# Summing over partitions on GpSimd instead of TensorE in the second stage of a gated feed-forward kernel

## The chip, the cores and the metric

The kernel runs on one core of one Trainium2 chip. Its time is the device time of one execution in microseconds (us); the profile shows one such execution, engine by engine: PE is TensorE, DVE is VectorE, ACT is ScalarE, POOL is GpSimd, SP is SyncE, which here only issues transfers.

## The reference

```
xr = x.reshape(B, T, 8, 128)                       # B, T = 4, 1024
h = gelu(einsum('btel,elf->btef', xr, W1) + b1)    # 8 groups, 128 -> 512
y = (einsum('btef,efl->btel', h, W2) + b2).reshape(B, T, 1024)
scale, shift = split(silu(emb) @ emb_W + emb_b, 2)
mu  = mean(y, axis=-1)
var = mean(square(y - mu), axis=-1)
hn  = ((y - mu) * rsqrt(var + 1e-5) * ln_g + ln_b) * (1 + scale) + shift
out = x + silu(hn) @ out_W + out_b
```

All is float32. A float32 product is done as three products of rounded halves (high x high, high x low, low x high), so that operands are split into a high and a low part first.

## The kernel before, in words

Stage one (to about 367 us) works on 32 items of 1024 tokens of one group: the two small products, Gelu between them, and a store of y to memory, transposed so that the 1024 features of a token lie over 128 partitions times 8 groups.

Stage two works on 16 blocks p of 256 tokens. A block is a tile `yb` of 128 partitions x 8 groups x 256 tokens; there are three such tiles, used in turn. The mean and the variance of a token are sums over 8 groups and 128 partitions. The sum over groups is a tree of three additions on DVE into a tile `total` of 128 x 256 (`mean_sum_first`, `mean_sum_rest`, L540 to L550; for the squares `var_sum_first`, `var_sum_rest`, L567 to L573). The sum over partitions is a product on PE with a 128 x 128 tile `ones_r` that holds 1/1024, so that every partition gets the mean (L780, L781, `row_sum`). Since the product takes rounded operands, DVE first splits `total` into `sum_hi` and `sum_lo` (`mean_split_up` L554 and L556, `var_split_up` L577 and L579).

The loop over i runs on each engine in an order written out by hand, with semaphores between engines. In step i:

- PE does projections q = 2i and 2i + 1 (128 tokens each, 48 products of 512 columns, L847) on block i. Behind the last group of the first it puts the mean product of block i + 2, behind the second the variance product of block i + 2. A projection waits for `finish(q - 2)`, since it writes the PSUM pair that this frees, and for `s_lo` of its block.
- DVE, in this order: `finish(2i - 1)` (L694: projection + residual), the reciprocal of the standard deviation of block i + 1 (L588), its two halves of `norm` (L593), the tree of the mean of block i + 2 and its split, `rest_s` (L611: the low part of the activations, first half), `finish(2i)`, `centre` of block i + 2 (L562, subtracts the mean, two halves), `rest_s` second half, the tree of the variance of block i + 2 and its split.
- ACT: Silu of block i + 1 (L456), its rounding (L387), the squares of block i + 2 (L382), the table of the square root (L390), the square root (L396), the table of Silu (L464).
- GpSimd adds the output bias to a residual tile, q = 2i and 2i + 1 (L343). Add q waits for projection q - 1 to be done and for the load of the residual; `finish(q)` waits for it.

Blocks 0 and 1 take their sums in stage one, and the change leaves them as they are; blocks 2 to 15, 14 of them, take theirs in steps 0 to 13.

Of the kernel before, what the change touches and what calls it, by code (L numbers as in the profile page):

```python
# [5 lines left out]
P = 128  # L6
F32 = mybir.dt.float32
F32R = mybir.dt.float32r
ALU = mybir.AluOpType
ACT = mybir.ActivationFunctionType  # L10
# [5 lines left out]
def cond_ffn_program(nc, x, xT, vectors, W1, W2, emb_W, out_W, out_b, out):  # L16
    B, T, D = x.shape
# [6 lines left out]
    TP = 2 * P  # L24
    NP = B * T // TP
    PT = TA // TP
    QN = 2 * NP
    HG = G // 2
# [6 lines left out]
    N = len(ORDER)  # L35
# [18 lines left out]

    MEAN_ITEM = {23: 0, 25: 1}
    VAR_ITEM = {26: 0, 28: 1}
    MEAN_OF = {(p - 2, 0, 7): p for p in range(2, NP)}
    VAR_OF = {(p - 2, 1, 7): p for p in range(2, NP)}

    def act_rounds(m):  # L60
        return m % C in (3, 0)
# [14 lines left out]
    with ExitStack() as ctx:  # L76
# [3 lines left out]
        def at(name, shape, offset, dt=F32):  # L80
            return nc.alloc_sbuf_tensor_at(name, shape, dt, offset=BASE + offset)
# [4 lines left out]
        psum = ctx.enter_context(nc.psum_tensor("psum", [P, 8, BANK], F32))  # L86
# [4 lines left out]
        S0 = 64 * KB  # L91
# [11 lines left out]
        eps = at("eps", [P, 1], S0 + 5312)  # L103
        sum_hi = at("sum_hi", [P, TP], S0 + 5632, F32R)
        sum_lo = at("sum_lo", [P, TP], S0 + 6656, F32R)
        std = at("std", [P, TP], S0 + 7680)
        total = at("total", [P, TP], S0 + 8704)
        total1 = at("total1", [P, TP], S0 + 9728)
        rstd0 = at("rstd0", [P, TP], S0 + 1536)
        R0 = S0 + 10752  # L110

# [19 lines left out]
        sq = at("sq", [P, G, TP], R0 + 112 * KB)  # L132
# [85 lines left out]
        def proj(q):  # L218
            return pair(2 * (q % 2))

        mean_ps = psum[:, 4, 0:TP]
        rstd_ps = psum[:, 5, 0:TP]
        var_ps = psum[:, 7, 0:TP]

        def half_of(h):
            return slice(h * HG, (h + 1) * HG)
# [100 lines left out]
        @block.gpsimd  # L327
        def _(pool):
            nc.gpsimd.memset(ident[:], 0.0).then_inc(ident_zeroed, 1)
            pool.wait_ge(ident_zeroed, 1)  # L330
            nc.gpsimd.affine_select(out=ident[:], in_=ident[:], compare_op=ALU.not_equal, fill=1.0,
                                    base=0, pattern=[[-1, P]], channel_multiplier=1).then_inc(ident_ready, 1)

            pool.wait_ge(out_b_landed, 16)
            for q in range(QN):
                if q == 0:
                    pool.wait_ge(rstd_done, 2)
                else:  # L340
                    pool.wait_ge(proj_done, q)
                pool.wait_ge(res_landed[q % 4], 16 * (q // 4 + 1))
                nc.gpsimd.tensor_tensor(res[:, q % 4], res[:, q % 4], out_b_all[:], ALU.add).then_inc(res_biased, 1)  # L343

        @block.scalar
        def _(act):
# [39 lines left out]
                    act.wait_ge(proj_done, 2 * p - 2)  # L386
                nc.scalar.copy(s_hi[p % 2][:, half_of(h)], yb[p % 3][:, half_of(h)]).then_inc(shi_done, 1)  # L387

            def root(p, var):
                nc.scalar.preload_act_table(ACT.Sqrt)  # L390
                if p < 2:
                    act.wait_ge(var_copied, p + 1)
                act.wait_ge(var_done, p + 1)
                if p >= 1:
                    act.wait_ge(rstd_done, p)
                nc.scalar.activation(std[:], var, ACT.Sqrt, bias=eps[:]).then_inc(std_done, 1)  # L396

            def tanh_y0(h):
                act.wait_ge(y0_halved, (h + 1) * HG)
# [50 lines left out]
            for i in range(NP - 1):  # L450
                p = i + 1
                for h in range(2):
                    act.wait_ge(normed, 2 * p + h + 1)
                    for g in range(h * HG, (h + 1) * HG):
                        b = p // PT
                        nc.scalar.activation(yb[p % 3][:, g], yb[p % 3][:, g], ACT.Silu, scale=mod_a[:, b, g:g + 1],  # L456
                                             bias=mod_c[:, b, g:g + 1]).then_inc(silu_done, 1)
                    act.wait_ge(silu_done, G * i + (h + 1) * HG)
                    round_s(p, h)
                if p + 1 < NP:  # L460
                    square(p + 1, 0)
                    square(p + 1, 1)
                    root(p + 1, var_ps)
                    nc.scalar.preload_act_table(ACT.Silu)  # L464

        @block.vector
        def _(dve):
# [75 lines left out]
            def total_of(p):  # L543
                return (total1 if p == 1 else total)[:]

            def mean_sum_rest(p):
                dve.wait_ge(mean_tree, 3 * p + 1)
                nc.vector.tensor_tensor(sq[:, 0:2], sq[:, 0:2], sq[:, 2:4], ALU.add).then_inc(mean_tree, 1)
                dve.wait_ge(mean_tree, 3 * p + 2)
                nc.vector.tensor_tensor(total_of(p), sq[:, 0], sq[:, 1], ALU.add).then_inc(mean_tree, 1)  # L550

            def mean_split_up(p):
                dve.wait_ge(mean_tree, 3 * p + 3)
                nc.vector.tensor_copy(sum_hi[:], total_of(p)).then_inc(mean_split, 1)  # L554
                dve.wait_ge(mean_split, 2 * p + 1)
                nc.vector.tensor_tensor(sum_lo[:], total_of(p), sum_hi[:].bitcast(F32), ALU.subtract  # L556
                                        ).then_inc(mean_split, 1)

            def centre(p, h, mean):
                dve.wait_ge(mean_done, p + 1)  # L560
                part = yb[p % 3][:, half_of(h)]
                nc.vector.tensor_tensor(part, part, mean.unsqueeze(1).to_broadcast([P, HG, TP]), ALU.subtract  # L562
                                        ).then_inc(centred, 1)
# [5 lines left out]
            def var_sum_rest(p):  # L569
                dve.wait_ge(var_tree, 3 * p + 1)  # L570
                nc.vector.tensor_tensor(sq[:, 0:2], sq[:, 0:2], sq[:, 2:4], ALU.add).then_inc(var_tree, 1)
                dve.wait_ge(var_tree, 3 * p + 2)
                nc.vector.tensor_tensor(total_of(p), sq[:, 0], sq[:, 1], ALU.add).then_inc(var_tree, 1)  # L573

            def var_split_up(p):
                dve.wait_ge(var_tree, 3 * p + 3)
                nc.vector.tensor_copy(sum_hi[:], total_of(p)).then_inc(var_split, 1)  # L577
                dve.wait_ge(var_split, 2 * p + 1)
                nc.vector.tensor_tensor(sum_lo[:], total_of(p), sum_hi[:].bitcast(F32), ALU.subtract  # L579
                                        ).then_inc(var_split, 1)  # L580

            def copy_var(p, var):
# [113 lines left out]
            for i in range(NP):  # L696
                p, ahead = i + 1, i + 2
                if i > 0:
                    finish(2 * i - 1)
                if p < NP:  # L700
                    invert(p, rstd_ps)
                    norm(p, 0, rstd_ps)
                    norm(p, 1, rstd_ps)
                if ahead < NP:
                    mean_sum_first(ahead)
                    mean_sum_rest(ahead)
                    mean_split_up(ahead)
                if p < NP:
                    rest_s(p, 0)
                finish(2 * i)  # L710
                if ahead < NP:
                    centre(ahead, 0, mean_ps)
                    centre(ahead, 1, mean_ps)
                if p < NP:
                    rest_s(p, 1)
                if ahead < NP:
                    var_sum_first(ahead)
                    var_sum_rest(ahead)
                    var_split_up(ahead)
            dve.wait_ge(res_biased, QN)  # L720
            for h in range(2):
                half = slice(h * BANK, (h + 1) * BANK)
# [5 lines left out]
        def _(pe):  # L728
# [54 lines left out]
            def mean_of(p, ps):  # L783
                pe.wait_ge(mean_split, 2 * p + 2)
                row_sum(ps).then_inc(mean_done, 1)

            def var_of(p, ps):
                pe.wait_ge(var_split, 2 * p + 2)
                row_sum(ps).then_inc(var_done, 1)
# [73 lines left out]
            for i in range(NP):  # L863
                for t in range(2):
                    q = 2 * i + t
                    if q >= 2:
                        pe.wait_ge(out_ready, q - 1)
                    else:
                        pe.wait_ge(gelu_done, M - 1 + q)
                    if q == QN - 1:  # L870
                        project_halves(q)
                        continue
                    for g in range(G):
                        if t == 0 and g % HG == 0:
                            pe.wait_ge(slo_done, 2 * i + g // HG + 1)
                        project(q, g)
                        if (i, t, g) in MEAN_OF:
                            if i == 0:
                                pe.wait_ge(y_staged, N)
                            mean_of(MEAN_OF[i, t, g], mean_ps)  # L880
                        if (i, t, g) in VAR_OF:
                            var_of(VAR_OF[i, t, g], var_ps)

# [30 lines left out]
```

## Time and profile before

| | |
|---|---|
| median of 3 runs | 727.7 us (727.65 to 727.92) |
| profiled execution, its own time | 727.84 us |
| its span | 726.0 us |
| PE busy | 720.6 us (99%) |
| DVE busy | 552.2 us (76%) |
| ACT busy | 453.1 us (62%) |
| GpSimd busy | 77.9 us (11%) |

The span is what the profile shows between the first and the last instruction; the execution's own time is 1.84 us longer. Busy shares are means over both stages.

### The profile page before, as it was taken

The page shows a single profiled execution, that of the slowest core. Times are in us where ns is not written, and L with a number is a line of the kernel's source. Part 1 is how long each engine was busy: PE and PEld are TensorE (multiplying, and loading weights), DVE is VectorE, ACT ScalarE, POOL GpSimd, SP SyncE. Part 2 cuts the span into 40 slices and gives each one's busy share as a digit, 9 for nine tenths or more (in the row PEclk, how much of TensorE's full clock was granted, in tenths as well). Part 3 has the DMA queues.
Part 4 walks back from the last instruction along what each step waited for, and adds up shares of the span by engine and source line. Part 5 has one row for each costly group of instructions (what it writes and reads, how often), then busy time and mean ns, then how long its engine had stood idle before and what let it go on. Part 6 is the DMA issues. An engine that isn't in the chain of part 4 may idle for free.

```text
span 726.0 us, 8305 instructions
## 1 busy us (share of the span) xinstructions
PE 720.6 (99%) x3208; PEld 585.6 (81%) x3208; DVE 552.2 (76%) x627; ACT 453.1 (62%) x494; POOL 77.9 (11%) x38
## 2 busy tenths in 40 slices
PE   8999999999999999999999999999999999999998
PEld 5887778777787888888878888888888888888886
DVE  6887888788776788889887778778778777787521
ACT  7786777767777788897865455554456453555500
POOL 0000000000000000000021221212212212122121
PEclk9999999999999999999999999999999999999999
DMA  6335366554542713323173433334332344332221
GB/s 234 110 124 187 115 219 196 181 155 164 203 152 81 261 62 113 102 72 117 59 272 133 172 117 146 116 144 175 142 148 95 137 174 170 120 117 87 87 88 58
DMA packets 42471, 101.78 MB, mean 140 GB/s; under 512 B 3136, under 2 KB 23616, under 8 KB 39360
## 3 DMA queue, kind: packets, MB, share of 16 engines
q1 hardware_dynamic: 41760, 100.73, 39.3%
q10 hardware_dynamic: 672, 0.52, 0.2%
q8 instruction: 25, 0.41, 0.2%
q14 instruction: 14, 0.11, 0.0%
HBM read 67.69 MB, written 33.55 MB: 139 GB/s over the span
## 4 chain that ended last, share of the span: by engine, by line
PE 98%; DMA 1%; DVE 0%; ACT 0%; issue 0%; ACTq 0%
PE psum L847 47%; PE psum L740 24%; PE psum L756 24%; PE psum L859 2%; PE psum L766 1%; DMA wraw<-in_W 1%; PE psum L781 1%; PE psum L780 1%; PE psum L803 0%; DVE g_lo L515 0%; ACT g_hi L368 0%; DVE W L491 0%; DVE res L724 0%; DVE W L489 0%; PE psum L776 0%
## 5 line engine op out<-in xcount | busy, mean ns | idle before, releaser
L515 DVE TENSOR_TENSOR g_lo<-g_raw,g_hi 128x1024 fp32r<-128x1024 f32 x128 | 156.7, 1225 | 61.3 <-ACT g_hi L368 59.0
L362 ACT ACTIVATE g_raw<-psum,cols 128x1024 f32<-128x1024 f32 x128 | 142.8, 1117 | 60.3 <-PE psum L740 51.4
L847 PE MATMUL psum<-oW_hi,s_hi 128*128 128x512 f32 x496 | 153.1, 390 | 0.0
L847 PE MATMUL psum<-oW_lo,s_hi 128*128 128x512 f32 x496 | 153.0, 389 | 0.0
L847 PE MATMUL psum<-oW_hi,s_lo 128*128 128x512 f32 x496 | 152.8, 389 | 0.0
L343 POOL TENSOR_TENSOR res<-res,out_b_all 128x1024 f32<-128x1024 f32 x32 | 77.2, 2413 | 635.7 <-DMA res<-in_x 372.9
L740 PE MATMUL psum<-xT_hi,W 128*128 128x512 f32 x508 | 137.2, 392 | 0.2
L756 PE MATMUL psum<-g_hi,W 128*128 128x512 f32 x512 | 137.3, 390 | 0.0
L740 PEld LDWEIGHTS psum<-xT_hi,W 128*128 128x128 f32 x508 | 94.2, 188 | 26.6 <-issue 7.7
L756 PEld LDWEIGHTS psum<-g_hi,W 128*128 128x128 f32 x512 | 95.9, 188 | 20.7 <-DVE yb L562 0.5
L847 PEld LDWEIGHTS psum<-oW_lo,s_hi 128*128 128x128 f32 x496 | 93.1, 188 | 19.7
L847 PEld LDWEIGHTS psum<-oW_hi,s_lo 128*128 128x128 f32 x496 | 93.1, 188 | 19.6
L847 PEld LDWEIGHTS psum<-oW_hi,s_hi 128*128 128x128 f32 x496 | 91.2, 188 | 17.2
L694 DVE TENSOR_TENSOR res<-psum,res 128x1024 f32<-128x1024 f32 x31 | 38.0, 1225 | 87.0 <-PE psum L847 87.0
L456 ACT ACTIVATE yb<-yb,mod_c,mod_a 128x256 f32<-128x256 f32 x120 | 62.4, 590 | 31.0 <-DVE yb L593 31.0
L756 PE MATMUL psum<-g_lo,W 128*128 128x512 f32 x256 | 79.0, 390 | 0.1
L740 PE MATMUL psum<-xT_lo,W 128*128 128x512 f32 x254 | 78.3, 389 | 0.0
L368 ACT CAST g_hi<-g_raw 128x1024 fp32r<-128x1024 f32 x64 | 67.2, 1050 | 11.0 <-PE psum L756 10.1
L382 ACT ACTIVATE sq<-yb 128x1024 f32<-128x1024 f32 x32 | 34.0, 1062 | 45.9 <-DVE yb L562 45.0
L756 PEld LDWEIGHTS psum<-g_lo,W 128*128 128x128 f32 x256 | 47.8, 188 | 10.6 <-DVE g_lo L515 0.9
L740 PEld LDWEIGHTS psum<-xT_lo,W 128*128 128x128 f32 x254 | 47.7, 188 | 10.1
L396 ACT ACTIVATE std<-psum,eps 128x256 f32<-128x256 f32 x14 | 6.7, 478 | 76.7 <-PE psum L781 76.7
(80 smaller groups left out, 605.6 us busy)
## 6 DMA issues: line engine op xcount, KB each, us to landing
y_scratch<-y_stage SPq DMA_DIRECT2D x32, 512.0 KB, 3.1
yb<-y_scratch SPq DMA_DIRECT2D x16, 1024.0 KB, 4.8
res<-in_x SPq DMA_DIRECT2D x32, 512.0 KB, 5.4
xT_raw<-in_xT SPq DMA_DIRECT2D x31, 512.0 KB, 4.4
out<-res SPq DMA_DIRECT2D x31, 512.0 KB, 2.8
emb_raw<-in_emb_W SPq DMA_DIRECT2D x8, 1024.0 KB, 7.5
wraw<-in_out_W SPq DMA_DIRECT2D x16, 256.0 KB, 5.0
wraw<-in_W SPq DMA_DIRECT2D x14, 256.0 KB, 4.8
```

Source lines behind the costliest of these rows:

```text
L343: nc.gpsimd.tensor_tensor(res[:, q % 4], res[:, q % 4], out_b_all[:], ALU.add).then_inc(res_biased, 1)
L362: nc.scalar.activation(g_raw[:, m % 2], ring(m), ACT.Gelu, bias=cols[:, R_B1 + k:R_B1 + k + 1]).then_inc(gelu_done, 1)
L368: nc.scalar.copy(g_hi[:, m % 2], g_raw[:, m % 2]).then_inc(ghi_act, 1)
L382: nc.scalar.activation(sq[:, half_of(h)], yb[p % 3][:, half_of(h)], ACT.Square).then_inc(squared, 1)
L456: nc.scalar.activation(yb[p % 3][:, g], yb[p % 3][:, g], ACT.Silu, scale=mod_a[:, b, g:g + 1], bias=mod_c[:, b, g:g + 1]).then_inc(silu_do ...
L515: nc.vector.tensor_tensor(g_lo[:, m % 2], g_raw[:, m % 2], g_hi[:, m % 2].bitcast(F32), ALU.subtract).then_inc(glo_done, 1)
L694: nc.vector.tensor_tensor(res[:, q % 4], proj(q), res[:, q % 4], ALU.add).then_inc(out_ready, 1)
L740: mm = nc.tensor.matmul(ring(m)[:, half], W[:, g % WS, w, cut], v[:, n % 2, half], start=(k == 0), stop=(k == 2))
L756: mm = nc.tensor.matmul(y_psum(n)[:, half], W[:, g % WS, w, cut], v[:, m % 2, half], start=(c == 0 and k == 0), stop=(c == C - 1 and k == 2))
L766: mm = nc.tensor.matmul(small(n)[32 * j:32 * j + 32], cond_silu[:, r], emb_raw[:, j * BANK:(j + 1) * BANK], start=True, stop=True, tile_po ...
L847: mm = nc.tensor.matmul(proj(q)[:, half], v[:, g, cut], w[:, g, half], start=(g == 0 and k == 0), stop=(g == G - 1 and k == 2))
L859: mm = nc.tensor.matmul(proj(q)[:, half], v[:, g, cut], w[:, g, half], start=(g == 0 and k == 0), stop=(g == G - 1 and k == 2))
```

## The change

The sums over partitions of blocks 2 to 15 are done by GpSimd, one instruction for the mean and one for the variance of a block: `partition_all_reduce` reads `total` (128 x 256) and writes the sum over all 128 partitions into every partition of a new tile `mean_all` or `var_all`. The 28 pairs of products with ones on PE and the 28 splits on DVE in stage two are gone. The division by 1024 goes into the instructions that use the sums: `centre` becomes one `scalar_tensor_tensor` (sum times -1/1024, plus y), the square root takes a scale of 1/1024. The variance tree of blocks 2 to 15 writes to `total1`, so that it doesn't overwrite the mean's `total`.

```diff
-            for q in range(QN):
+            def add_bias(q):
                 if q == 0:
                     pool.wait_ge(rstd_done, 2)
                 else:
                     pool.wait_ge(proj_done, q)
                 pool.wait_ge(res_landed[q % 4], 16 * (q // 4 + 1))
                 nc.gpsimd.tensor_tensor(res[:, q % 4], res[:, q % 4], out_b_all[:], ALU.add).then_inc(res_biased, 1)
+            def mean_all_of(p):
+                pool.wait_ge(mean_tree, 3 * p + 3)
+                if p == 2:
+                    pool.wait_ge(var_done, 2)
+                if p >= 3:
+                    pool.wait_ge(centred, 2 * p)
+                nc.gpsimd.partition_all_reduce(mean_all[:], total[:], P, bass.bass_isa.ReduceOp.add
+                                               ).then_inc(mean_done, 1)
+            def var_all_of(p):
+                pool.wait_ge(var_tree, 3 * p + 3)
+                if p >= 3:
+                    pool.wait_ge(std_done, p)
+                nc.gpsimd.partition_all_reduce(var_all[:], total1[:], P, bass.bass_isa.ReduceOp.add
+                                               ).then_inc(var_done, 1)
+            for i in range(NP):
+                add_bias(2 * i)
+                if i + 2 < NP:
+                    mean_all_of(i + 2)
+                add_bias(2 * i + 1)
+                if i + 2 < NP:
+                    var_all_of(i + 2)
...
-                    root(p + 1, var_ps)
+                    root(p + 1, var_all[:], 1.0 / D)
...
+            def centre_all(p, h):
+                dve.wait_ge(mean_done, p + 1)
+                part = yb[p % 3][:, half_of(h)]
+                nc.vector.scalar_tensor_tensor(part, mean_all[:].unsqueeze(1).to_broadcast([P, HG, TP]), -1.0 / D, part,
+                                               ALU.mult, ALU.add).then_inc(centred, 1)
...
-                    mean_split_up(ahead)
...
-                    centre(ahead, 0, mean_ps)
-                    centre(ahead, 1, mean_ps)
+                    centre_all(ahead, 0)
+                    centre_all(ahead, 1)
...
-                    var_split_up(ahead)
...
-                        if (i, t, g) in MEAN_OF:
-                            if i == 0:
-                                pe.wait_ge(y_staged, N)
-                            mean_of(MEAN_OF[i, t, g], mean_ps)
-                        if (i, t, g) in VAR_OF:
-                            var_of(VAR_OF[i, t, g], var_ps)
```

```order
L329 MEMSET ident 128x128
L331 ISA
L331 AFFINE_SELECT ident<-ident 128x128
L343 TENSOR_TENSOR res<-res,out_b_all 128x1024 x32
L76 UNCONDITIONAL_BRANCH
```

And here is the same place of the changed program, with step 0 and the start of step 1; the rows ISA with operands are the two partition sums:

```order
L329 ISA
L329 AFFINE_SELECT ident<-ident 128x128
L340 TENSOR_TENSOR res<-res,out_b_all 128x1024
L348 ISA
L348 ISA mean_all<-total 128x256
L340 ISA
L340 TENSOR_TENSOR res<-res,out_b_all 128x1024
L355 ISA
L355 ISA var_all<-total_67 128x256
L340 ISA
L340 TENSOR_TENSOR res<-res,out_b_all 128x1024
```

Ahead of each partition sum there now stands an instruction that names library 1, and ahead of the addition behind it one that names library 0 again: four such instructions in each of the steps 0 to 13, 56 in all, each ahead of the semaphore waits of the instruction that it serves.

On DVE one step of stage two reads, before:

```order
L694 TENSOR_TENSOR res<-psum,res 128x1024
L562 TENSOR_TENSOR yb<-yb,psum 128x1024 x2
L611 TENSOR_TENSOR s_lo<-yb,s_hi 128x1024
L567 TENSOR_TENSOR sq<-sq 128x1024
L571 TENSOR_TENSOR sq<-sq 128x512
L573 TENSOR_TENSOR total<-sq 128x256
L577 CAST sum_hi<-total 128x256
L579 TENSOR_TENSOR sum_lo<-total,sum_hi 128x256
L694 TENSOR_TENSOR res<-psum,res 128x1024
```

and in the changed program:

```order
L725 TENSOR_TENSOR res<-psum,res 128x1024
L587 SCALAR_TENSOR_TENSOR yb<-mean_all,yb 128x1024 x2
L642 TENSOR_TENSOR s_lo<-yb,s_hi 128x1024
L598 TENSOR_TENSOR sq<-sq 128x1024
L602 TENSOR_TENSOR sq<-sq 128x512
L604 TENSOR_TENSOR total<-sq 128x256
L725 TENSOR_TENSOR res<-psum,res 128x1024
```

Only the split and the operand of `centre` differ; the order on DVE is the same.

## Rows read from the trace of the kernel before

**Rows 1.** The page: busy time and instructions; granted clock in forty slices, tenths
```profile
PE 720.6 (99%) x3208; PEld 585.6 (81%) x3208; DVE 552.2 (76%) x627; ACT 453.1 (62%) x494; POOL 77.9 (11%) x38
...
PEclk9999999999999999999999999999999999999999
```

**Rows 2.** Who waited for whom, GpSimd's queue, 400 to 700 us
```profile
POOL res L343 <- PE psum L847: 235.8, 27, 8.7
```

**Rows 3.** Timeline of PE around one variance product: start, duration, line
```profile
522.93 0.28 PE L780 MATMUL psum<-sum_hi,ones_r 128*128 128x256 f32 x1
523.05 0.28 PE L781 MATMUL psum<-sum_lo,ones_r 128*128 128x256 f32 x1
523.16 0.63 PE L847 MATMUL psum<-oW_hi,s_hi 128*128 128x512 f32 x2
```

**Rows 4.** Timeline of GpSimd, the first addition and four of the last
```profile
374.36 2.49 POOL L343 TENSOR_TENSOR res<-res,out_b_all 128x1024 f32<-128x1024 f32 x1 [372.89 <-DMA res<-in_x]
...
668.00 2.41 POOL L343 TENSOR_TENSOR res<-res,out_b_all 128x1024 f32<-128x1024 f32 x1 [8.73 <-PE psum L847]
679.14 2.40 POOL L343 TENSOR_TENSOR res<-res,out_b_all 128x1024 f32<-128x1024 f32 x1 [8.73 <-PE psum L847]
690.28 2.42 POOL L343 TENSOR_TENSOR res<-res,out_b_all 128x1024 f32<-128x1024 f32 x1 [8.74 <-PE psum L847]
701.16 2.40 POOL L343 TENSOR_TENSOR res<-res,out_b_all 128x1024 f32<-128x1024 f32 x1 [8.46 <-PE psum L847]
```

**Rows 5.** The chain that ended last, its last pieces: start, us, line, instructions
```profile
668.15 10.91 PE psum L847 x48
...
711.96 10.89 PE psum L859 x48
```

**Rows 6.** Timeline of DVE and ACT in one step, 500 to 524 us
```profile
502.00 1.75 DVE L588 RECIPROCAL psum<-std 128x256 f32<-128x256 f32 x1
503.78 2.35 DVE L593 TENSOR_TENSOR yb<-yb,psum 128x1024 f32<-128x1024 f32 x2
508.03 0.43 DVE L550 TENSOR_TENSOR total<-sq 128x256 f32<-128x256 f32 x1
508.49 0.29 DVE L554 CAST sum_hi<-total 128x256 fp32r<-128x256 f32 x1
508.82 0.43 DVE L556 TENSOR_TENSOR sum_lo<-total,sum_hi 128x256 fp32r<-128x256 f32 x1
513.13 2.34 DVE L562 TENSOR_TENSOR yb<-yb,psum 128x1024 f32<-128x1024 f32 x2
514.38 2.19 ACT L382 ACTIVATE sq<-yb 128x1024 f32<-128x1024 f32 x2 [3.11 <-DVE yb L562]
518.59 0.42 DVE L573 TENSOR_TENSOR total<-sq 128x256 f32<-128x256 f32 x1
523.37 0.48 ACT L396 ACTIVATE std<-psum,eps 128x256 f32<-128x256 f32 x1 [5.49 <-PE psum L781]
```

**Rows 7.** Timeline of GpSimd at the start of the program
```profile
0.73 0.20 POOL L329 MEMSET ident<- 128x128 f32 x1 [0.29 <-POOLq L905]
1.17 0.29 POOL L331 TENSOR_SCALAR_AFFINE_SELECT ident<-ident 128x128 f32<-128x128 f32 x1 [0.23 <-POOL ident L329]
```

**Rows 8.** Groups of instructions by line, 400 to 730 us: busy us, mean ns
```profile
L694 DVE TENSOR_TENSOR res<-psum,res 128x1024 f32<-128x1024 f32 x29 | 35.5, 1225 | 83.8 <-PE psum L847 83.8
L390 ACT ACT_TABLE_LOAD x13 | 16.7, 1283 | 0.2
```

**Rows 9.** Transfers: issues, KB each, median us from issue to landing
```profile
emb_raw<-in_emb_W SPq DMA_DIRECT2D x8, 1024.0 KB, 7.5
out_b_all<-in_out_b SPq DMA_DIRECT2D x1, 512.0 KB, 5.9
cols<-in_vectors SPq DMA_DIRECT2D x1, 52.0 KB, 4.5
```

**Rows 10.** The instruction of the new centring's form in stage one, by its line
```profile
L606 DVE SCALAR_TENSOR_TENSOR yb<-tanh,yb x2: 1218/1219/1220, 347.9 to 355.6; 128x1024 f32<-128x1024 f32 x2
```

More of the change, by code:

```diff
@@ L56, in cond_ffn_program @@
     VAR_ITEM = {26: 0, 28: 1}
-    MEAN_OF = {(p - 2, 0, 7): p for p in range(2, NP)}
-    VAR_OF = {(p - 2, 1, 7): p for p in range(2, NP)}
     def act_rounds(m):
@@ L109, in cond_ffn_program @@
         rstd0 = at("rstd0", [P, TP], S0 + 1536)
+        mean_all = at("mean_all", [P, TP], S0 + 5632)
+        var_all = at("var_all", [P, TP], S0 + 6656)
         R0 = S0 + 10752
@@ L219, in proj @@
             return pair(2 * (q % 2))
-        mean_ps = psum[:, 4, 0:TP]
         rstd_ps = psum[:, 5, 0:TP]
-        var_ps = psum[:, 7, 0:TP]
         def half_of(h):
@@ L332, in _ @@
                                     base=0, pattern=[[-1, P]], channel_multiplier=1).then_inc(ident_ready, 1)
-            pool.wait_ge(out_b_landed, 16)
-            for q in range(QN):
+            def add_bias(q):
                 if q == 0:
@@ L343, in _ @@
                 nc.gpsimd.tensor_tensor(res[:, q % 4], res[:, q % 4], out_b_all[:], ALU.add).then_inc(res_biased, 1)
+            def mean_all_of(p):
[12 more added lines that the diff above has]
+                                               ).then_inc(var_done, 1)
+            pool.wait_ge(out_b_landed, 16)
+            for i in range(NP):
[5 more added lines that the diff above has]
+                    var_all_of(i + 2)
         @block.scalar
@@ L387, in round_s, with root @@
                 nc.scalar.copy(s_hi[p % 2][:, half_of(h)], yb[p % 3][:, half_of(h)]).then_inc(shi_done, 1)
-            def root(p, var):
+            def root(p, var, scale=1.0):
                 nc.scalar.preload_act_table(ACT.Sqrt)
@@ L395, in root @@
                     act.wait_ge(rstd_done, p)
-                nc.scalar.activation(std[:], var, ACT.Sqrt, bias=eps[:]).then_inc(std_done, 1)
+                nc.scalar.activation(std[:], var, ACT.Sqrt, bias=eps[:], scale=scale).then_inc(std_done, 1)
             def tanh_y0(h):
@@ L544, in total_of, with var_total_of @@
                 return (total1 if p == 1 else total)[:]
+            def var_total_of(p):
+                return (total if p == 0 else total1)[:]
             def mean_sum_rest(p):
@@ L572, in var_sum_rest @@
                 dve.wait_ge(var_tree, 3 * p + 2)
-                nc.vector.tensor_tensor(total_of(p), sq[:, 0], sq[:, 1], ALU.add).then_inc(var_tree, 1)
+                nc.vector.tensor_tensor(var_total_of(p), sq[:, 0], sq[:, 1], ALU.add).then_inc(var_tree, 1)
             def var_split_up(p):
                 dve.wait_ge(var_tree, 3 * p + 3)
-                nc.vector.tensor_copy(sum_hi[:], total_of(p)).then_inc(var_split, 1)
+                nc.vector.tensor_copy(sum_hi[:], var_total_of(p)).then_inc(var_split, 1)
                 dve.wait_ge(var_split, 2 * p + 1)
-                nc.vector.tensor_tensor(sum_lo[:], total_of(p), sum_hi[:].bitcast(F32), ALU.subtract
+                nc.vector.tensor_tensor(sum_lo[:], var_total_of(p), sum_hi[:].bitcast(F32), ALU.subtract
                                         ).then_inc(var_split, 1)
```

## The prediction

> **What bounds the kernel now.** I read the page's busy line first. PE is busy in 720.6 of 726.0 us, and its granted clock is the upper level, 2.4 GHz, in all forty slices [rows 1]. The chain that ended last is then read from its end: it is one projection behind the other, 10.91 us each with 48 products, to the last product at 722.85 [rows 5]. The waits of GpSimd show the other side: its additions wait for PE, 27 times up to 8.7 us [rows 2]. So only PE counts before, and a GpSimd addition starts each time a projection ends: 11.14 us apart where a product with ones stands behind the projection (668.00 to 679.14), 10.88 us where none does (690.28 to 701.16) [rows 4]. A step of two projections lasts 22.28 us.
>
> **What is removed.** On PE 28 pairs of products with ones. The pair starts at 522.93 and the next projection at 523.16 [rows 3], 0.23 us; by the spacing of the additions a pair costs 11.14 - 10.88 = 0.26 us. I take 0.26: 28 x 0.26 = 7.3 us, all of it on the path that sets the end. This is all that can be won: the time would be 727.84 - 7.3 = 720.5 us, and a step 21.76 us. On DVE the splits go, 0.29 + 0.43 us a sum [rows 6]; DVE waits for PE by 83.8 us in the stage [rows 8], so this is worth nothing to the end, and only makes `total` the last thing a sum waits for, 0.75 us sooner. The new form of `centre` costs 1.22 us a half by its like in stage one [rows 10], against 1.17 before [rows 6]: nothing. The scale in the square root is in the same instruction.
>
> **What is added, on GpSimd.** Per step it now has two additions, two partition sums, and four changes of library, since the additions and the sums stand in different ones. None of this can overlap on GpSimd itself, which works its queue in order. So its step is 2 x A + 2 x M + 4 x R, and it decides the time once that is more than 21.76 us.
>
> A, an addition, is 2.41 us [rows 4].
>
> M, a partition sum of 128 x 256, stands in no row. Below it lies the reading of 256 columns at the rate of the addition, 2.41 x 256 / 1024 = 0.6 us. Above it I put seven such passes, as if 128 partitions were folded in half seven times: 4.2 us. Nearest is the addition itself, four such passes; I take M = 2.4.
>
> R, a change of library, stands in no row either. Below lies the one instruction of this kind that the trace has: the mask starts 0.23 us after the tile ahead of it is done, with such an instruction between them [rows 7]. But that names library 0, which may already be there, and nothing before named another. ACT's change of tables takes 1.28 us [rows 8]. But code of a library has to come from memory, and everything that comes from memory here takes longer: 52 KB land in 4.5 us, 4 KB spread to all partitions (512 KB in all) in 5.9, 1 MB in 7.5 [rows 9]. Nearest is the second of them, one source that goes to many places, as a library goes to all of GpSimd's cores. I take R = 5.9, with 4.5 and 7.5 as ends for a change that does load, and 0.23 for one that doesn't.
>
> The Trainium skill ("GPSIMD Engine Reference", section Instruction dispatch) says that the first call into a freshly loaded library pays about 6 us that show as no instruction of their own. The row of the trace above shows 0.23 us and doesn't bear this out, but may hold no load. By the page's 5.95 us a step would last 33.4 us and the time would be about 872 us; by 0.23 it would be 720.5.
>
> **The sum.** A GpSimd step is 2 x 2.41 + 2 x 2.4 + 4 x 5.9 = 33.2 us against the 21.76 that PE needs. So GpSimd becomes the bound in steps 0 to 13. Does it wait for the others within its step? Between a mean and its variance stand centring 2.34, two squares 2.19 and the tree of 2.4 (as long as that from 506.1 to 508.5), some 7 us, while GpSimd changes, adds and changes back, 5.9 + 2.4 + 5.9 = 14.2 us. Between a variance and the next mean stand the root 0.48, the reciprocal 1.75, `norm` 2.35 and the tree 2.4, also 7 us against 14.2 [rows 6]. Both are hidden, so its queue runs without gaps. (If the load starts only after the semaphore wait, the cover is 5.9 + 2.4 = 8.3 us, and still enough.)
>
> Addition 0 starts at 374.36 [rows 4], when its residual has landed, and this stays. Addition 28 is the first behind the last step with sums: it starts at 374.36 + 14 x 33.2 = 839.2. From there PE sets the end again. Additions 28 to 31 need no change. Addition 28 takes 2.4, `finish(28)` 1.23 [rows 8], which frees PSUM for projection 30; projections 30 and 31 take 2 x 10.9 (29 has already run, since PE runs ahead of the additions), and the tail behind the last product is 726.0 - 722.85 = 3.15 [rows 5]. That is 839.2 + 28.6 = 867.8 us of span, and with the 1.84 us around it 869.6. The profiled execution lies 0.1 us above the median of 727.7, so I say **870 us**, 20% slower. In general the time is 404.8 + 14 steps of GpSimd.
>
> **What is late next.** In a slow step PE works 21.8 of 33.2 us and idles the rest, in pieces of some 4 to 5 us: a projection waits for the `finish` that waits for an addition, and its second half for `rest_s`, which on DVE stands behind `centre` and so behind the mean. DVE stands queued behind `centre` and behind the reciprocal.
>
> **The rivals.**
> Faster: *the change of library costs little*, because both libraries stay resident or are fetched ahead. It decides at 4 x R = 21.76 - 9.6, so R = 3.0 us. At R = 1.28, in the step from 500.90: addition to 503.3, change to 504.6, mean from 508.5 (when `total` is done [rows 6]) to 510.9, before `centre` would start at 513.13; change, addition from 512.2, change, variance from 519.0 to 521.4, before the root's 523.37. Nothing is late, and the 7.3 us remain: 720.5 us. For it speaks only the 0.23 us of [rows 7]. Chance 0.08. A near balance, within 0.2%, needs R at 3.0 to 3.2: 0.02.
>
> *The partition sum is slow.* If a core folds its 16 partitions one after the other, at 0.6 us a pass, M is 9.6 us, the step 4.8 + 19.2 + 23.6 = 47.6 us, and the time 404.8 + 14 x 47.6 = 1071 us. No row speaks for or against. The Trainium skill ("GPSIMD Engine Reference", section Cross-partition) gives 247.7 us for a reduction over partitions of 2048 columns; if this instruction went at that rate, an estimate of 31 us for 256 columns would make the time about 1670 us. No trace here shows it, and the page speaks of another instruction. Chance 0.06.
>
> *PE's clock falls.* Its granted clock is full in all rows, but PE has no gaps there. If with gaps it stood at 1.2 GHz throughout, a projection would take 21.8 us, a step 43.6, and 32 projections at 10.9 us more each would make the time 720.5 + 349, about 1070 us. It needs more than 16 us a projection to matter at all, since GpSimd leaves PE 33.2 us for two. Chance 0.04.
>
> **How the numbers follow.** GpSimd as the bound, with R from 4.5 to 7.5 and M from 0.6 to 4.2, has 0.84. Its ends: R = 4.5 with M = 0.6 is a step of 24.0 and 741 us; R = 7.5 with M = 4.2 is a step of 43.2 and 1010 us. As the corners are less likely than the middle, some 0.02 lies in them below 745. The range 745 to 1010 leaves out the faster case (0.08), the balance (0.02), that corner and the two slow rivals (0.10), some 0.2. A measurement of this kernel tells 0.2% from no change. Faster 0.08, same 0.02, slower 0.90.
>
> **What would show it.** Right: GpSimd's rows of L340, L348 and L355 stand some 33 us apart per step, with 5 to 7 us of idle time ahead of each that ends with no other engine; PE in the second half of the span idles a third of the time and waits for DVE; only the 4 pairs of products with ones of blocks 0 and 1 are left. Wrong: additions still 10.9 us apart with PE behind them (the changes are cheap), or rows of L348 and L355 that themselves last over 5 us (the sum is the cost, not the change), or PE busy with long products at a lower granted clock.

## The result and the profile after

The changed kernel takes 899.7 us (897.14 to 901.17) against 727.7 us: 1.236 times as long, 95% interval 1.234 to 1.237. The forecast was 870 us, with a range of 745 to 1010. The profiled execution took 901.17 us, its span is 899.1 us.

The page of the changed kernel: busy time by engine, and the slices. The rows answer to [rows 1].

```profile
PE 765.0 (85%) x3152; PEld 606.1 (67%) x3152; DVE 540.9 (60%) x571; ACT 453.1 (50%) x494; POOL 135.4 (15%) x66
...
PE   9999999999999999997685866866866867768678
...
PEclk9999999999999999999988988978989879889779
...
DMA packets 42471, 101.78 MB, mean 113 GB/s; under 512 B 3136, under 2 KB 23616, under 8 KB 39360
```

Stage one is as it was. In stage two PE, which was never idle, has gaps, and GpSimd is shown busy for 15% only. That 15% misleads: what GpSimd does between its rows stands in the idle column. The waits of the changed kernel, the longest first, behind that of stage one for the first residual (engine and line, what it waited for, total us, times, longest):

```profile
...
POOL res L340 <- issue: 201.1, 28, 7.7
ACT std L418 <- POOL var_all L355: 174.7, 14, 13.2
...
PE psum L876 <- DVE res L725: 103.0, 21, 7.2
...
DVE yb L587 <- POOL mean_all L348: 85.8, 14, 6.6
POOL mean_all L348 <- issue: 83.1, 14, 6.1
POOL var_all L355 <- issue: 77.5, 13, 6.2
DVE res L725 <- POOL res L340: 73.1, 24, 4.3
```

In the steps GpSimd waits for no engine: "issue" is time for which the profile has no releaser. Before, its additions waited 27 times for PE [rows 2]; now ACT, DVE and PE wait for it or for what it holds up. The timeline of GpSimd in one step, to be read against [rows 4]:

```profile
622.39 2.33 POOL L340 TENSOR_TENSOR res<-res,out_b_all 128x1024 f32<-128x1024 f32 x1 [6.93 <-issue]
630.60 1.81 POOL L348 PARTITION_ALL_REDUCE mean_all<-total  x1 [5.88 <-issue]
639.46 2.39 POOL L340 TENSOR_TENSOR res<-res,out_b_all 128x1024 f32<-128x1024 f32 x1 [7.05 <-issue]
647.87 1.81 POOL L355 PARTITION_ALL_REDUCE var_all<-total  x1 [6.02 <-issue]
656.64 2.34 POOL L340 TENSOR_TENSOR res<-res,out_b_all 128x1024 f32<-128x1024 f32 x1 [6.97 <-issue]
```

A step lasts 34.3 us here (622.39 to 656.64), and only 8.3 us of it are work. About 5.9 us lie ahead of each partition sum and 7.0 ahead of each addition, which is where the program has its changes of library. The instructions that name a library are in the trace too, two records a change, but they are not counted as busy: at most 0.1 us each, and the 6 to 7 us come behind them. GpSimd's groups by line, all 14 steps, and the records of the 28 changes ahead of additions:

```profile
L340 POOLq MODIFY_POOL_CONFIG  x56: 98/98/98, 385.4 to 859.3; - x56
L340 POOL TENSOR_TENSOR res<-res,out_b_all 128x1024 f32<-128x1024 f32 x32 | 84.0, 2628 | 584.8 <-DMA res<-in_x 373.8 <-issue 201.1 <-PE psum L876 9.8
L355 POOL PARTITION_ALL_REDUCE var_all<-total x14 | 25.3, 1810 | 83.2 <-issue 77.5 <-DMA res<-in_x 5.7
L348 POOL PARTITION_ALL_REDUCE mean_all<-total x14 | 25.3, 1809 | 83.1 <-issue 83.1
```

The one row of "DMA", 5.7 us, is a change like the others (5.73 us ahead of the last sum). A change to library 1 costs 83.1 / 14 = 5.94 us, one to library 0 201.1 / 28 = 7.18 us, a sum 1.81 us, an addition 2.63 us. That makes a step of 2 x (5.94 + 7.18 + 1.81 + 2.63) = 35.1 us. From the first addition to the 29th, the first behind the last step with sums, it is 866.88 - 375.47 = 491.4 us, 14 times 35.1:

```profile
375.47 2.41 POOL L340 TENSOR_TENSOR res<-res,out_b_all 128x1024 f32<-128x1024 f32 x1 [373.76 <-DMA res<-in_x]
...
866.88 8.32 POOL L340 TENSOR_TENSOR res<-res,out_b_all 128x1024 f32<-128x1024 f32 x3 [7.56 <-issue]
```

### The profile page after: what moved, and what is told of

The parts are those of the page before. It is cut to its first block, busy times and chain, and to the rows that moved or that the text cites. A ratio compares the mean times of both kernels' runs of the same rounds, so it can differ in the third digit from the quotient of the medians.

```text
span 899.1 us, 8303 instructions
## 1 busy us (share of the span) xinstructions
PE 765.0 (85%) x3152; PEld 606.1 (67%) x3152; DVE 540.9 (60%) x571; ACT 453.1 (50%) x494; POOL 135.4 (15%) x66
## 2 busy tenths in 40 slices
DMA packets 42471, 101.78 MB, mean 113 GB/s; under 512 B 3136, under 2 KB 23616, under 8 KB 39360
## 4 chain that ended last, share of the span: by engine, by line
PE 47%; issue 35%; POOL 10%; DVE 5%; ACT 2%; DMA 1%; POOLq 0%; SPq 0%; DVEq 0%; ACTq 0%
PE psum L769 17%; PE psum L785 17%; PE psum L876 11%; POOL res L340 6%; POOL mean_all L348 3%; POOL var_all L355 2%; DVE g_lo L537 1%; PE psum L888 1%; DMA res<-in_x 1%; PE psum L795 1%; ACT g_raw L384 1%; DVE res L725 1%; ACT g_hi L390 1%; DVE yb L587 1%; DMA wraw<-in_W 0%
## 5 line engine op out<-in xcount | busy, mean ns | idle before, releaser
L876 PE MATMUL psum<-oW_hi,s_hi 128*128 128x512 f32 x496 | 174.6, 436 | 128.6 <-DVE res L725 103.0
L876 PEld LDWEIGHTS psum<-oW_hi,s_hi 128*128 128x128 f32 x496 | 100.2, 209 | 164.1 <-DVE res L725 113.4
L340 POOL TENSOR_TENSOR res<-res,out_b_all 128x1024 f32<-128x1024 f32 x32 | 84.0, 2628 | 584.8 <-DMA res<-in_x 373.8
L876 PE MATMUL psum<-oW_lo,s_hi 128*128 128x512 f32 x496 | 166.8, 420 | 0.0
L876 PE MATMUL psum<-oW_hi,s_lo 128*128 128x512 f32 x496 | 164.5, 415 | 0.0
L876 PEld LDWEIGHTS psum<-oW_lo,s_hi 128*128 128x128 f32 x496 | 103.1, 208 | 24.1
L876 PEld LDWEIGHTS psum<-oW_hi,s_lo 128*128 128x128 f32 x496 | 101.4, 205 | 23.3
L418 ACT ACTIVATE std<-var_all,eps 128x256 f32<-128x256 f32 x14 | 7.1, 510 | 174.7 <-POOL var_all L355 174.7
L619 DVE RECIPROCAL psum<-std 128x256 f32<-128x256 f32 x15 | 26.4, 1762 | 98.6 <-ACT std L418 98.6
L587 DVE SCALAR_TENSOR_TENSOR yb<-mean_all,yb 128x1024 f32<-128x1024 f32 x28 | 33.1, 1222 | 85.8 <-POOL mean_all L348 85.8
L390 ACT CAST g_hi<-g_raw 128x1024 fp32r<-128x1024 f32 x64 | 67.2, 1050 | 10.9 <-PE psum L785 9.8
```

The source lines that it names most:

```text
L390: nc.scalar.copy(g_hi[:, m % 2], g_raw[:, m % 2]).then_inc(ghi_act, 1)
L587: nc.vector.scalar_tensor_tensor(part, mean_all[:].unsqueeze(1).to_broadcast([P, HG, TP]), -1.0 / D, part, ALU.mult, ALU.add).then_inc(cen ...
L876: mm = nc.tensor.matmul(proj(q)[:, half], v[:, g, cut], w[:, g, half], start=(g == 0 and k == 0), stop=(g == G - 1 and k == 2))
```

## The experiments

Theory A is that of the prediction: GpSimd's queue is the bound, and the changes of library fill it. Theory B: the sums themselves, or the way to GpSimd and back. Theory C: PE, with its gaps and its lower clock.

**No additions on GpSimd, so no changes in the loop.** DVE adds the bias, GpSimd does nothing but the 28 sums (the lines with a minus and the loop are GpSimd's, the rest DVE's).

```diff
-            def add_bias(q):
...
+            for p in range(2, NP):
+                mean_all_of(p)
+                var_all_of(p)
...
+            def add_bias(q):
...
+                nc.vector.tensor_tensor(res[:, q % 4], res[:, q % 4], out_b_all[:], ALU.add).then_inc(res_biased, 1)
...
+                add_bias(2 * i)
                 finish(2 * i)
...
                     var_sum_rest(ahead)
+                add_bias(2 * i + 1)
```

Expected: 

> The additions of the output bias go from GpSimd to DVE (32 of 128x1024, some 1.22 us each), so that GpSimd does nothing in stage two but the 28 partition sums, and its library changes once. Theory A (the four changes of library per step are the cost): GpSimd works 2 x 1.81 us per step of 21.8, PE is the bound again, and the 0.26 us of each of the 28 products with ones are won: 720.5 to 722 us, faster than before. Theory B (the sum itself, or the way to GpSimd and back, holds up DVE and ACT): the step stays longer than 22.3 us and the time above 728 us.

Measured: 720.6 us (720.51 to 720.9), ratio to before 0.990, interval 0.989 to 0.991. It beats both kernels. GpSimd's timeline of this kernel, with what it waited for:

```profile
505.63 2.70 POOL L340 PARTITION_ALL_REDUCE mean_all<-total  x1 [8.75 <-DVE total L562]
515.94 2.70 POOL L347 PARTITION_ALL_REDUCE var_all<-total  x1 [7.62 <-DVE total L591]
527.39 2.70 POOL L340 PARTITION_ALL_REDUCE mean_all<-total  x1 [8.75 <-DVE total L562]
```

A step is 21.76 us (505.63 to 527.39), the 22.28 of before less 2 x 0.26. The same 28 sums cost nothing here, so theory B falls: the way to GpSimd and back fits under PE's work.

**The changes alone.** The kernel before, sums on TensorE, with a change to library 1 and back ahead of additions 1 to 28; library 1 is never called.

```diff
...
             for q in range(QN):
+                if 1 <= q <= QN - 4:
+                    nc.gpsimd.load_library(library_config.all_libraries[1])
```

Expected: 

> The kernel before, with sums on TensorE as they were, and a change to library 1 and back to library 0 ahead of the additions 1 to 28; nothing of library 1 is called. Theory A, with each change paid where it stands: an addition with its two changes lasts 2.5 + 5.9 + 7.1 = 15.5 us against the 10.9 of a projection, so 375 + 28 x 15.5 + 28.6 + 1.9, about 840 us. Theory A', a change is paid by the first call into the library: 2.4 + 7.1 = 9.5 us, under a projection, about 728 us. Theory B (the sums): 728 us.

Measured: 854.9 us (853.57 to 856.13), interval of the ratio 1.172 to 1.176. The group of its additions:

```profile
L346 POOL TENSOR_TENSOR res<-res,out_b_all 128x1024 f32<-128x1024 f32 x32 | 77.1, 2412 | 763.7 <-issue 384.0 <-DMA res<-in_x 372.7 <-PE psum L850 7.0
```

A pair of changes takes 384.0 / 28 = 13.7 us, against 5.94 + 7.18 = 13.1 in the changed kernel. Every second pair takes some 14.8 us, the others some 12.7; in a long one the load of the residual ends inside it (at 517.09, 4.2 us ahead of the addition at 521.30), so that the longer pairs may hold more than the changes. Even a shorter one with its addition, 15.1 us, exceeds the 10.9 us of a projection. So a change is paid where it stands, whether the library is called or not, and the changes alone cost 127 us, against 172 us for the whole change.

**Two changes in a step instead of four.** GpSimd's order becomes addition, addition, mean, variance.

```diff
                 add_bias(2 * i)
+                add_bias(2 * i + 1)
                 if i + 2 < NP:
                     mean_all_of(i + 2)
-                add_bias(2 * i + 1)
-                if i + 2 < NP:
                     var_all_of(i + 2)
```

Expected: 

> The changed kernel with GpSimd's order in a step as addition, addition, mean, variance: two changes of library in a step instead of four, the same sums. GpSimd now waits between the mean and the variance for centring, squares and the tree, some 5.9 us. Theory A: a step is 2 x 2.5 + 2 x 1.81 + 5.9 + 7.1 + 5.9 = 27.5 us instead of 35, so about 800 us. Theory B: as many sums and a longer wait between them, so 900 us or more.

Measured: 814.0 us (812.14 to 815.92), interval of the ratio 1.116 to 1.120. GpSimd's timeline:

```profile
503.33 1.81 POOL L348 PARTITION_ALL_REDUCE mean_all<-total  x1 [6.25 <-issue]
511.16 1.79 POOL L355 PARTITION_ALL_REDUCE var_all<-total  x1 [6.02 <-DVE total L603]
521.13 4.75 POOL L340 TENSOR_TENSOR res<-res,out_b_all 128x1024 f32<-128x1024 f32 x2 [8.18 <-issue]
532.06 1.81 POOL L348 PARTITION_ALL_REDUCE mean_all<-total  x1 [6.18 <-issue]
```

The step is 28.7 us (503.33 to 532.06). The wait between the sums, 6.02 us, was hidden in the changed kernel and is now in the open, and still the time falls by 86 us. The change back took 8.2 us here, 1.1 more than expected, which is about the 14 us above the 800 expected.

**Every sum twice.** A spare sum ahead of each, into another tile.

```diff
...
+                nc.gpsimd.partition_all_reduce(again[:], total[:], P, bass.bass_isa.ReduceOp.add
+                                               ).then_inc(again_done, 1)
+                pool.wait_ge(again_done, 2 * (p - 2) + 0 + 1)
                 nc.gpsimd.partition_all_reduce(mean_all[:], total[:], P, bass.bass_isa.ReduceOp.add
...
```

Expected: 

> The changed kernel with each of the 28 partition sums done twice, first into a spare tile, then as before; no further change of library. Theory A (GpSimd's queue is the bound): each spare sum adds its 1.81 us and about 0.1 us for the wait on it, 28 x 1.9 = 53 us, so about 953 us. The price of the sums themselves is then 28 x 1.8 = 51 us of what GpSimd does, a small part of the loss. Theory C (PE with its gaps and lower clock is the bound, GpSimd has slack): 900 to 910 us.

Measured: 951.9 us (949.72 to 954.14), 52 us above the changed kernel. What is put into GpSimd's queue shows in the time in full, and all 28 sums are worth as much as these: 52 of its 491 us.

**Fewer products on PE.** The projections 0 to 30 leave out the products of high activations with low weights.

```diff
-                for k, (v, w) in enumerate(((s_hi[s], oW_hi), (s_hi[s], oW_lo), (s_lo[s], oW_hi))):
+                for k, (v, w) in enumerate(((s_hi[s], oW_hi), (s_lo[s], oW_hi))):
...
```

Expected: 

> The changed kernel without the products of the high activations with the low weights in the projections 0 to 30 (a third of each is left out, so the output is less exact): PE needs 7.3 us a projection instead of 10.9. Theory A: GpSimd's step of 35 us stays, only the projection behind its last sum gets shorter, by 3.6 us, so about 893 us. Theory C: the time falls by a large part of 31 x 3.6 = 112 us, to 800 or 850 us.

Measured: 892.7 us (891.74 to 893.61), 7.0 us less. The windows view from 420 to 860 us, for the changed kernel (PE, PEld, DVE, ACT, POOL busy; granted clock; share of the DMA engines; GB/s):

```profile
420.00:860.00 440.00, 320.42 (x1216) 250.24 (x1215) 202.82 (x188) 140.07 (x185) 111.67 (x51) 0.88 0.24 87
```

and for the one with fewer products:

```profile
420.00:860.00 440.00, 251.72 (x816) 190.53 (x816) 203.97 (x189) 140.87 (x186) 110.78 (x50) 0.77 0.23 87
```

PE has a third less to do and a lower clock, and the other engines do as much in the same 440 us: theory C falls.

**Naming the library that is there.** The kernel before with two instructions that name library 0 ahead of additions 1 to 28.

```diff
...
+                if 1 <= q <= QN - 4:
+                    for _ in range(2):
+                        nc.gpsimd.load_library(library_config.all_libraries[0])
```

Expected: 

> The kernel before with two instructions that name library 0 ahead of each of the additions 1 to 28, while library 0 is the one that is there. Theory A with a check of what is resident (the 0.23 us of the mask): nothing is loaded, 728 us. Theory A with a load each time: an addition lasts 2.4 + 2 x 6.9 = 16.2 us against 10.9 of a projection, so about 860 us.

Measured: 728.1 us (727.76 to 729.8), interval of the ratio 0.999 to 1.001: no difference. The 0.23 us of [rows 7] fit this.

**Half of the change, three times.** Means on GpSimd, variances on TensorE as before.

```diff
...
                 if i + 2 < NP:
                     mean_all_of(i + 2)
                 add_bias(2 * i + 1)
-                if i + 2 < NP:
-                    var_all_of(i + 2)
...
+                        if (i, t, g) in VAR_OF:
...
+                            var_of(VAR_OF[i, t, g], var_ps)
```

Expected: 

> Half of the change: the means on GpSimd, the variances on TensorE with their splits on DVE as before. Two changes of library in a step. Theory A: GpSimd needs 2 x 2.5 + 1.81 + 5.9 + 7.1 = 19.8 us a step, under the 22.0 that PE needs with one product with ones, so PE is the bound and 14 x 0.26 = 3.6 us are won: 724 us. If a change is only paid once the wait of the sum is over, the mean comes 5.9 us later and still in time: 724 as well, with 5.9 us between the total and the sum in the trace. Theory B: half of the loss stays, 800 us or more.

Measured: 727.3 us (725.99 to 730.33), interval of the ratio 0.9985 to 1.0007: not told from before, and 3 us short of what was expected. The steady part is as expected: PE is busy without a gap from 420 to 720 us. The loss is one row in the waits of PE:

```profile
PE psum L802 <- DVE sum_lo L602: 1.9, 1, 1.9
```

It is the variance product of step 0, and behind it the products run at 1.2 GHz for a few us (granted clock 0.50 of full speed from 393 to 396 us). The mean of block 2 came late, since the first addition waits for its residual to 375.5 us and the change of library follows. The next run was to mend that (lines against the run before):

```diff
+            mean_all_of(2)
             pool.wait_ge(out_b_landed, 16)
...
-                if i + 2 < NP:
+                if 0 < i and i + 2 < NP:
                     mean_all_of(i + 2)
```

Expected: 

> The means on GpSimd and the variances on TensorE, as in the run before, but the first mean, of block 2, stands ahead of the first addition, so that library 1 is loaded in stage one. Theory: the 3.6 us that were expected were lost at the start, where the first variance's product waited 1.9 us for its total and the clock fell behind that wait; with the first mean 8 us sooner nothing waits, so 724 us and no spread of the runs. If the loss lies elsewhere: 727 us again.

Measured: 735.8 us (734.98 to 737.73), interval of the ratio 1.009 to 1.012: slower by 1%. The mean was in time, at 376.07, but the addition behind it now had the change ahead of it. DVE's `finish(0)` waits for that addition, and `centre` stands behind `finish(0)`:

```profile
375.85 1.22 DVE L635 TENSOR_TENSOR s_lo<-yb,s_hi 128x1024 fp32r<-128x1024 f32 x1
388.49 1.22 DVE L718 TENSOR_TENSOR res<-psum,res 128x1024 f32<-128x1024 f32 x1 [11.42 <-POOL res L341]
389.63 5.49 DVE L580 SCALAR_TENSOR_TENSOR yb<-mean_all,yb 128x1024 f32<-128x1024 f32 x2
```

So PE waited 9.2 us at the same place. Expecting the mean to be what is late was wrong by half: in step 0 either the mean or the addition comes behind a change. The third run leaves step 0 as it was before the change and starts with block 3 (lines against the first of the three):

```diff
+    MEAN_OF = {(0, 0, 7): 2}
...
-                if i + 2 < NP:
+                if 0 < i and i + 2 < NP:
                     mean_all_of(i + 2)
...
+                if ahead == 2:
+                    centre(ahead, 0, mean_ps)
+                    centre(ahead, 1, mean_ps)
+                elif ahead < NP:
```

Expected: 

> The means of blocks 3 to 15 on GpSimd, that of block 2 and all variances on TensorE. Step 0 is then as before, with no change of library in it; from step 1 on GpSimd needs 19.8 us a step. Theory: what the two runs with the means alone lost lies in step 0, where everything is late by the load of the first residual, so without it 13 x 0.26 = 3.4 us are won: 724.4 us. If the loss lies in the steady steps: 727 us or more.

Measured: 724.5 us (724.25 to 725.85), interval of the ratio 0.9945 to 0.9972. So two changes in a step, some 14 us here, are free when GpSimd's step stays under PE's 22 us, and only step 0 had no room for them.

## Why the prediction was right, and where its sizes were off

**PE loses 28 pairs at 0.26 us, 7.3 us in all: right.** The kernel with DVE's additions has exactly this gain: 727.8 - 7.3 = 720.5, measured 720.6.

**GpSimd becomes the bound, since its step is longer than PE's 21.76 us: right.** The doubled sums (+52 us), the halved changes (-86 us) and the fewer products (-7 us) all say so. In the two profiles, the fewer products take 4.0 us from the end, where projection 30 alone stands behind the last sum. From the 14 steps, with a third of PE's work gone, they take 2.1 us: a step lasts 34.95 us instead of 35.1. The rest is the first addition, 1.5 us sooner. The chain that ended last could be read otherwise: in the steps six of its pieces, 81 us, lie on PE. One of them:

```profile
609.04 11.23 PE psum L876 x48
620.27 2.12 issue
622.39 0.18 POOL res L340
```

Each of the six ends 2.1 to 2.5 us before the addition that the chain puts behind it, while the change ahead of that addition is under way, and these changes are as long as the others (6.9 to 7.6 us). So PE was not what came last there.

**The step's size: 33.2 forecast, 35.1 measured**, by terms:

- *Changes, 4 x 5.9 = 23.6: measured 26.2.* A change to library 1 fits the 5.9 us taken from a transfer's row [rows 9], one to library 0 takes 7.2. That the first fits to 0.04 us is luck: the row is of a load of the bias, and no run shows what a change of library loads or how. This is the mis-sized term: 2.6 us a step, 37 us in 14 steps. The Trainium skill's about 6 us ("GPSIMD Engine Reference", section Instruction dispatch) agrees with the 5.94 us of a change to library 1. That it comes with the first call does not: in the run with changes alone nothing of library 1 was called, and the pair cost 13.7 us.
- *Sums, 2 x 2.4 = 4.8: measured 3.6.* This takes back 1.2 us a step of what the changes lack, which is luck too.
- *Additions, 2 x 2.41 = 4.8: measured 5.3*, by what the last section tells.

So 14 x 1.9 = 27 us come from the step. Another 1.1 us is the first addition, at 375.47 instead of 374.36, and 3.6 us the end: 32.2 us from addition 28 on against 28.6, 3.1 of these 3.6 because projection 30 starts at the lower clock (14.02 us instead of 10.9). The last pieces of the chain that ended last show it beside [rows 5]:

```profile
846.17 18.22 PE psum L876 x72
870.95 14.02 PE psum L876 x48
884.97 10.89 PE psum L888 x48
```

27 + 1.1 + 3.6 are the 31 us between the span forecast, 867.8, and the 899.1 measured.

**The rest of the step is hidden behind the changes: right.** All idle time of GpSimd in the steps is of "issue" but for the one row of 5.7 us, and none is put down to DVE, ACT or PE.

**PE's gaps: right in kind.** It is idle 27% from 420 to 860 us, in pieces of up to 7.2 us where 4 to 5 were said. The clock does fall, which the rival had and the forecast left out of its sum. After a gap of 6.8 us PE's timeline reads, and the windows view gives the granted clock of the stretch (the 0.50 behind PE, PEld, DVE, ACT and POOL):

```profile
627.00 1.22 PE L876 MATMUL psum<-oW_hi,s_hi 128*128 128x512 f32 x2 [6.75 <-DVE res L725]
628.02 1.06 PE L876 MATMUL psum<-oW_lo,s_hi 128*128 128x512 f32 x2
628.87 1.06 PE L876 MATMUL psum<-oW_hi,s_lo 128*128 128x512 f32 x2
...
631.86 0.62 PE L876 MATMUL psum<-oW_hi,s_hi 128*128 128x512 f32 x2
632.32 0.63 PE L876 MATMUL psum<-oW_lo,s_hi 128*128 128x512 f32 x2
```
```profile
627.00:631.00 4.00, 4.00 (x9) 3.17 (x10) 0.00 (x0) 0.00 (x0) 0.40 (x1) 0.50 0.32 131
```

Pairs 0.85 us apart are the level of 1.2 GHz, 0.46 that of 2.4. A few us a step at the lower level don't reach the bound: the run with fewer products has a granted clock of 0.77 from 420 to 860 us, against 0.88, and its steps are no longer.

**The slow sum did not happen.** A sum takes 1.81 us for 256 columns. That is far from the estimate of 31 us by the figure of the Trainium skill ("GPSIMD Engine Reference", section Cross-partition), which is of another instruction.

**What stays open**: why the change to library 0 takes longer than that to library 1, and why it took 8.2 us in the run with two changes a step. The kernel's own transfers don't explain the first: from 615.47 to 622.39 us, a change to library 0, the DMA engines moved nothing, and it took 6.9 us all the same. The transfers behind a change show in no queue of the profile: the packets are 42471 in the changed kernel and in the run with changes alone.

## What to carry to other kernels

Before work is moved to GpSimd, list its instructions in order with the library of each: alternating between two libraries cost 6 to 8 us a change in these runs, naming the one that is there nothing. The profile shows that time as idle "issue" and an engine 15% busy, so look at the spacing of its rows and not at its share. Then keep one kind of work on it: here the sums stay and the additions go to DVE, which turns 24% slower into 1% faster.

## What the runs showed of the hardware

GpSimd and DVE hold each other up when a DVE instruction with two SBUF operands meets an addition on GpSimd: whichever starts second is stretched by nearly what is left of the first. In the changed kernel DVE's `rest_s`, 1.22 us alone, started while the addition ran from 622.39 to 624.72:

```profile
622.43 3.38 DVE L642 TENSOR_TENSOR s_lo<-yb,s_hi 128x1024 fp32r<-128x1024 f32 x1
```

In another step `rest_s` started first, and the addition, 2.38 us alone, was stretched:

```profile
444.88 1.22 DVE L642 TENSOR_TENSOR s_lo<-yb,s_hi 128x1024 fp32r<-128x1024 f32 x1
```
```profile
445.36 2.95 POOL L340 TENSOR_TENSOR res<-res,out_b_all 128x1024 f32<-128x1024 f32 x1 [7.44 <-issue]
```

The Trainium skill names this contention ("GPSIMD Engine Reference", section Specifications: the SBUF interfaces are shared, with contention for DVE instructions in a 2-port mode or with two SBUF inputs). The two cases above are of the second kind. Two operands in SBUF are not the whole of it: a cast with one was stretched as well, in the kernel before, from 0.29 us to 2.38 beside the first addition. `finish`, with one operand in PSUM and one in SBUF, was not, beside the additions from 866.88 to 875.20 of the changed kernel:

```profile
374.61 2.38 DVE L554 CAST sum_hi<-total 128x256 fp32r<-128x256 f32 x1
```
```profile
869.67 1.22 DVE L725 TENSOR_TENSOR res<-psum,res 128x1024 f32<-128x1024 f32 x1 [2.31 <-POOL res L340]
```

The sums are stretched too: 2.70 us in the kernel with DVE's additions, against 1.81. There `rest_s` starts 0.2 us ahead of each mean's sum, and the addition of the bias 0.2 us ahead of each variance's. But a sum holds DVE up for less than its length: DVE's addition at 506.59 took 2.12 us, 0.90 more than alone, with 1.7 us of the sum still to run. That this sharing is the cause was read from the timelines; no run took it away.

The kernel with DVE's additions has 11 us of idle time ahead of the mask, at the start of the program, and none of "issue" ahead of its first sum. That these 11 us are its one change of library is read from that, and no run shows it:

```profile
12.07 1.22 POOL L329 TENSOR_SCALAR_AFFINE_SELECT ident<-ident 128x128 f32<-128x128 f32 x1 [11.15 <-issue]
```

A change can run ahead of the semaphore wait of the sum behind it. With the means alone, one addition ended at 507.01 and the total was there at 512.16; the sum started 1.86 us later and not 5.9:

```profile
514.02 1.81 POOL L349 PARTITION_ALL_REDUCE mean_all<-total  x1 [7.01 <-issue]
```
